# An AdaLN-style recurrence with a quantised feed-forward on one core: the first input tiles and the last output tile in halves

## What is computed

```python
# conditioning: a recurrence over time; the program runs it over T = 2048 steps, batch 2
xW = einsum('ntd,dh->nth', x, Wx) + b
next_h = tanh(xw_t + prev_h @ Wh)            # h0 = cond, 512 wide

# feed-forward on all hidden states, quantised on the fly
xq = clip(round(x / s), 0, 255) * s          # s = max(x) / 255
wq = clip(round(w / s_w), -128, 127) * s_w   # s_w = max|w| / 127 for each output row
bq = round(b / (s * s_w)) * (s * s_w)
h = relu(einsum(xq, w1q) + b1q)              # 512 -> 2048
y = einsum(hq, w2q) + b2q                    # 2048 -> 512, h quantised in the same way
return x + y
```

## Time and profile before

| | us |
|---|---|
| median of 3 runs | 501.66 |
| lowest, highest | 497.53, 505.16 |
| the profiled execution | 500.23 |
| its span, from the first to the last instruction | 498.2 |

### The profile page before, as it was taken

How to read it: one execution, slowest core, us unless ns; L and a number is a source line. 1 busy time by engine, 2 the same in 40 slices (tenths; PEclk the granted TensorE clock), 3 DMA queues, 4 the chain that set the end, 5 groups by cost and what they waited for, 6 DMA issues and landing times.

```text
span 498.2 us, 8921 instructions
## 1 busy us (share of the span) xinstructions
PE 479.3 (96%) x3004; PEld 327.6 (66%) x3004; DVE 293.8 (59%) x511; ACT 243.5 (49%) x451; POOL 92.1 (18%) x69
## 2 busy tenths in 40 slices
PE   8999999999999999999669999999998999999996
PEld 3678888888999999999654444444443444444442
DVE  2798556458233354545779877778787343454442
ACT  0326454454233232323673555555545567766761
POOL 2833290400000000000000000000001344434244
PEclk9999999999999999999899999999998999999999
DMA  8974422200457000000002777000002189878883
GB/s 292 387 255 170 169 86 86 84 1 1 95 108 135 0 1 0 0 0 0 2 1 87 293 298 314 24 0 0 0 1 86 51 293 311 301 268 314 300 318 119
DMA packets 38167, 65.40 MB, mean 131 GB/s; under 512 B 19056, under 2 KB 19200, under 8 KB 34560
## 3 DMA queue, kind: packets, MB, share of 16 engines
q1 hardware_dynamic: 37472, 64.04, 37.5%
q10 hardware_dynamic: 576, 1.05, 0.6%
q0 software_dynamic: 96, 0.01, 0.0%
HBM read 39.93 MB, written 20.97 MB: 122 GB/s over the span
## 4 chain that ended last, share of the span: by engine, by line
PE 87%; DVE 7%; DMA 2%; issue 1%; ACT 1%; SPq 1%; DVEq 0%
PE bank L850 22%; PE bank L789 22%; PE bank L579 14%; PE bank L616 12%; PE bank L622 11%; PE bank L606 3%; DMA arena<-w 2%; PE bank L642 2%; DVE arena L1179 2%; DVE arena L1318 1%; ACT arena L1049 1%; DVE w_absmax L1172 1%; PE bank L569 1%; DVE late_max L1525 0%; SPq L419 0%
## 5 line engine op out<-in xcount | busy, mean ns | idle before, releaser
L555 POOL TENSOR_SCALAR arena<-arena,bq 128x512 f32<-128x512 f32 x32 | 49.8, 1574 | 343.2 <-DVEq L1595 284.9
L789 PE MATMUL bank<-arena,w_words 128*128 128x512 f16 (+1 forms) x512 | 110.7, 379 | 0.7 <-DVE arena L1416 0.7
L850 PE MATMUL bank<-arena,w2t 128*128 128x512 f16 x512 | 111.1, 379 | 0.0
L789 PEld LDWEIGHTS bank<-arena,w_words 128*128 128x128 f16 x512 | 50.0, 98 | 61.0 <-DVE arena L1416 1.5
L850 PEld LDWEIGHTS bank<-arena,w2t 128*128 128x128 f16 x512 | 49.5, 98 | 61.5 <-DVE arena L1572 2.5
L1505 DVE TENSOR_REDUCE acc_max<-arena 128x2 f32<-128x1024 f32 x60 | 72.3, 1217 | 20.1 <-ACT arena L1105 19.1
L1105 ACT COPY arena<-bank 128x1024 f32<-128x1024 f32 x56 | 56.7, 1012 | 44.6 <-PE bank L789 44.6
L1125 ACT ACTIVATE arena<-arena,bias,scale 128x512 uint16 (+1 forms) x93 | 69.0, 804 | 8.7 <-PE bank L850 6.6
L616 PE MATMUL bank<-arena 128*128 x512 | 63.5, 277 | 0.0
L622 PE MATMUL bank<-arena 128*128 x512 | 62.4, 275 | 0.0
L616 PEld LDWEIGHTS bank<-arena 128*128 128x128 f32 x512 | 59.7, 192 | 0.6 <-issue 0.4
(11 more groups left out here) (111 smaller groups left out, 378.3 us busy)
## 6 DMA issues: line engine op xcount, KB each, us to landing
spill<-arena SPq DMA_DIRECT2D x12, 1024.0 KB, 3.9
arena<-spill SPq DMA_DIRECT2D x12, 1024.0 KB, 7.9
arena<-w SPq DMA_DIRECT2D x8, 1024.0 KB, 5.3
arena<-x_t SPq DMA_DIRECT2D x32, 256.0 KB, 3.9
y_t<-arena SPq DMA_DIRECT2D x32, 256.0 KB, 2.1
arena<-x_t SPq DMA_DIRECT2D x7, 1024.0 KB, 8.2
arena<-x_t ACTq DMA_DIRECT2D x4, 256.0 KB, 5.7
arena<-wx SPq DMA_DIRECT2D x4, 256.0 KB, 5.2
```

The lines of the kernel that those rows point to most:

```text
L555: nc.gpsimd.tensor_scalar(xb[:, d], xb[:, d], bq2[:, d:d + 1], None, ALU.add).then_inc(xb_ready, 1)
L789: mm = nc.tensor.matmul(bank[:, f % 8, :], w1t[:, k, f * P:(f + 1) * P], states_in[:, k, :], start=(k == 0), stop=(k == KT - 1))
L850: return nc.tensor.matmul(bank[:, 4 + d, :], w2t[:, f, d * P:(d + 1) * P], hq[:, f % HQ_RING, :], start=(f == 0), stop=(f == FT - 1))
```

## The change

The first tile (k = 0) of Wx and of the first x group is loaded as two transfers of 256 columns each, with a semaphore for each half. TensorE multiplies the first half of the columns of x with all four parts of the Wx tile, then the second half. It makes five idle products instead of seven. At the end, the last group's products stand behind the loop (now of seven turns) as a copy of their own, in which the fourth output tile is accumulated as two halves of 256 columns, in banks 7 and 3; its last three products of the first half come before those of the second. VectorE scales and SP stores each half by itself.

```diff
+HALF_BANKS = (7, 3)
-IDLE_START = 7
+IDLE_START = 5
@@ SyncE
-            for k in range(KT):
+            for j in range(2):
+                nc.sync.dma_start(wx_sb[:, 0, j * HALF:(j + 1) * HALF],
+                                  wx_v[0, :, j * HALF:(j + 1) * HALF]).then_inc(wx_first[j], 16)
+            for k in range(1, KT):
                 nc.sync.dma_start(wx_sb[:, k, :], wx_v[k]).then_inc(wx_in[k], 16)
...
-            store(GROUPS - 1)
+            store(GROUPS - 1, KT - 1)
+            for half in range(2):
+                sp.wait_ge(y_ready, Y_RING + GROUPS * KT + half)
+                cols = slice(half * HALF, (half + 1) * HALF)
+                nc.sync.dma_start(yT_v[tokens(GROUPS - 1), KT - 1, :, cols],
+                                  xb[:, KT - 1, cols]).then_inc(y_stored[KT - 1], 16)
             for d in range(KT):
-                sp.wait_ge(y_stored[d], 16 * GROUPS)
+                sp.wait_ge(y_stored[d], 16 * (GROUPS + (d == KT - 1)))
@@ TensorE
-            for k in range(KT):
+            for t in range(2):
+                pe.wait_ge(x0_first[t], 16)
+                for j in range(KT):
+                    if t == 0 and j % 2 == 0:
+                        pe.wait_ge(wx_first[j // 2], 16)
+                    nc.tensor.matmul(bank[:, j, t * HALF:(t + 1) * HALF], wx_sb[:, 0, j * P:(j + 1) * P],
+                                     x_in[:, X_ORDER[0], 0, t * HALF:(t + 1) * HALF],
+                                     start=(t == 0), stop=False, skip_group_check=True)
+            for k in range(1, KT):
                 pe.wait_ge(wx_in[k], 16)
                 pe.wait_ge(x0_in[k], 16)
...
-            def second_product(g, f, d):
-                return nc.tensor.matmul(bank[:, 4 + d, :], w2t[:, f, d * P:(d + 1) * P],
-                                        hq[:, f % HQ_RING, :], start=(f == 0), stop=(f == FT - 1))
+            def second_product(g, f, d, split=False, halves=(0, 1)):
+                weights = w2t[:, f, d * P:(d + 1) * P]
+                if not split or d < KT - 1:
+                    return nc.tensor.matmul(bank[:, 4 + d, :], weights, hq[:, f % HQ_RING, :],
+                                            start=(f == 0), stop=(f == FT - 1))
+
+                for half in halves:
+                    mm = nc.tensor.matmul(bank[:, HALF_BANKS[half], 0:HALF], weights,
+                                          hq[:, f % HQ_RING, half * HALF:(half + 1) * HALF],
+                                          start=(f == 0), stop=(f == FT - 1))
+                return mm
...
-                for d in range(KT):
+                for d in range(KT - 1 if split else KT):
...
+                if split:
+                    for half in range(2):
+                        for f in range(FT - TOGETHER, FT):
+                            mm = second_product(g, f, KT - 1, split, halves=(half,))
+                        mm.then_inc(last_half, 1)
...
-            with pe.Fori(0, GROUPS) as g:
+            with pe.Fori(0, GROUPS - 1) as g:
                 second_products(g)
+            second_products(GROUPS - 1, split=True)
@@ ScalarE
-            for k in range(KT):
+            for t in range(2):
+                nc.scalar.dma_start(x_in[:, X_ORDER[0], 0, t * HALF:(t + 1) * HALF],
+                                    x0_v[0, :, t * HALF:(t + 1) * HALF]).then_inc(x0_first[t], 16)
+            for k in range(1, KT):
                 nc.scalar.dma_start(x_in[:, X_ORDER[0], k, :], x0_v[k]).then_inc(x0_in[k], 16)
@@ VectorE
-            for k in range(KT):
+            for j in range(2):
+                dve.wait_ge(wx_first[j], 16)
+            for k in range(1, KT):
                 dve.wait_ge(wx_in[k], 16)
...
-            output(GROUPS - 1, range(KT), last=True)
+            output(GROUPS - 1, range(KT - 1))
+            dve.wait_ge(xb_ready, GROUPS * KT)
+            for half in range(2):
+                dve.wait_ge(last_half, half + 1)
+                cols = slice(half * HALF, (half + 1) * HALF)
+                nc.vector.scalar_tensor_tensor(
+                    out=xb[:, KT - 1, cols], in0=bank[:, HALF_BANKS[half], 0:HALF],
+                    scalar=s2_bits[:, KT - 1:KT], in1=xb[:, KT - 1, cols], op0=ALU.mult,
+                    op1=ALU.add).then_inc(y_ready, 1)
```

More of the change, by code:

```diff
@@ L281, in rnn_ffn_program @@
         bank = ctx.enter_context(nc.psum_tensor("bank", [P, 8, 512], F32))
+        wx_first = [sem(f"wx_first{j}") for j in range(2)]
+        x0_first = [sem(f"x0_first{t}") for t in range(2)]
         wx_in = [sem(f"wx_in{k}") for k in range(KT)]
@@ L364, in rnn_ffn_program @@
         y_acc = sem("y_acc")
+        last_half = sem("last_half")
         y_half = sem("y_half")
@@ L489, in fetch, with store @@
                                       spill[s, :, n * piece:(n + 1) * piece]).then_inc(fetched[n], 16)
-            def store(g):
-                for d in range(KT):
+            def store(g, tiles=KT):
+                for d in range(tiles):
                     sp.wait_ge(y_ready, Y_RING + g * KT + d + 1)
@@ L664, in _ @@
                     mm = nc.tensor.matmul(bank[:, j, :], wx_sb[:, k, j * P:(j + 1) * P],
-                                          x_in[:, X_ORDER[0], k, :], start=(k == 0),
-                                          stop=(k == KT - 1))
+                                          x_in[:, X_ORDER[0], k, :], start=False,
+                                          stop=(k == KT - 1), skip_group_check=True)
                     if k == KT - 1:
@@ L858, in wait_hidden, with opening_products @@
                     pe.wait_ge(relu_ready, g * (FT - len(OWN)) + f - mine + 1)
-            def opening_products(g):
+            def opening_products(g, split):
                 for f in range(2):
@@ L870, in opening_products, with last_products @@
                 for f in range(2):
-                    second_product(g, f, KT - 1).then_inc(hq_used, 1)
-            def last_products(g):
-                for d in range(KT):
+                    second_product(g, f, KT - 1, split).then_inc(hq_used, 1)
+            def last_products(g, split):
+                for d in range(KT - 1 if split else KT):
                     for f in range(FT - TOGETHER, FT):
@@ L884, in last_products, with second_products @@
                         mm.then_inc(y_acc, 1)
-            def second_products(g):
-                opening_products(g)
+                if split:
[3 more added lines that the diff above has]
+                        mm.then_inc(last_half, 1)
+            def second_products(g, split=False):
+                opening_products(g, split)
                 for f in range(2, FT - TOGETHER):
@@ L890, in second_products @@
                     for d in range(KT):
-                        mm = second_product(g, f, d)
+                        mm = second_product(g, f, d, split)
                     mm.then_inc(hq_used, 1)
-                last_products(g)
-            with pe.Fori(0, GROUPS) as g:
+                last_products(g, split)
+            with pe.Fori(0, GROUPS - 1) as g:
                 second_products(g)
+            second_products(GROUPS - 1, split=True)
         @block.scalar
@@ L1544, in _, with output @@
                                     ALU.mult).then_inc(scales1_ready, 1)
-            def output(g, tiles, last=False):
+            def output(g, tiles):
                 for d in tiles:
                     dve.wait_ge(xb_ready, g * KT + d + 1)
-                    if d == KT - 1 and not last:
+                    if d == KT - 1:
                         dve.wait_ge(y_half, 1 + g + 1)
@@ L1554, in output @@
                         continue
[L1555 to L1558, removed]
+                    dve.wait_ge(y_acc, g * (KT - 1) + d + 1)
                     nc.vector.scalar_tensor_tensor(
```

## The result

| | median us | lowest, highest | runs |
|---|---|---|---|
| kernel before | 503.65 | 497.53, 506.20 | 22 |
| changed kernel | 505.93 | 503.05, 507.54 | 22 |

The ratio is 1.0074, interval 1.0049 to 1.0099: the changed kernel is slower, by 0.7%, within the 2% that I had forecast. (A ratio here is an estimate over the runs and not the quotient of the two medians; it can lie some tenths of a percent away from it.) The median of 505.93 us is outside my range (499.2 to 505.6). I had worked out +1.06 us; the medians are 2.3 us apart, the plain means (502.82 and 505.66) 2.8, and the ratio stands for 3.7. The kernel before, too, is not what its first three runs showed: of its 22 runs, 11 lie from 497.5 to 503.0 and 11 from 504.3 to 506.2. The changed kernel has no run under 503.

A forecast was written before the change was run, and what follows sets the result against it. The prediction took the chain from w1's first block through VectorE to p3(1), then TensorE, as the bound. Adding +0.96 us (collisions) and +0.1 (tail) to the 501.66 median gave 502.7 us, range 499.2 to 505.6.

The forecast's parts named there:

- What bounds the kernel: Early chain: w1's first block lands at 14.86, VectorE quantises, add_11(1) releases TensorE, which waits 0.89 us at p3(1).
- A start at 4.0, δ = 0.45: Head: TensorE starts 0.9 us earlier than 4.89; δ, its work's forward shift up to p3(1), is 0.45 us, bounds 0 and 0.55.
- ε: Head: delay of the landing of w1's first block caused by the split loads, 0.1 us, bounds 0 and 0.5.
- The collisions: Second block: each L1179 beginning after GpSimd's x_sums(3) starts costs 1.41 us, others 0.40; two collide, +0.96 us, chance 0.38.
- r: Second block: δ + ε, forecast 0.55; one collision under 0.22, two from 0.22 to 0.61, three from 0.61 to 1.0.
- my 35.7: Forecast start of p3(1) on TensorE, instead of 34.76, after a wait of 2.3 us.
- The clock: Rival: a gap at the start or the 2.3 us wait at p3(1) halves TensorE's clock, +1.7 us; chance 0.10.
- the four-collision case: Rival's extreme at the second L1179: all four operations collide with GpSimd, 4.23 − 0.5, giving 505.5 us.
- The tail: Kernel end: moving the last stores' 1 MB sets the end, so halving the last output tile costs +0.1 us.
- Hidden: Rival at the head: halves land hardly earlier, r under 0.22, giving 501.6 us; chance 0.27.
- first meeting turned: Rival in the first block: VectorE's L1179 starts before x_sums(2), one collision goes, −1.2 us, giving 500.4; chance 0.13.
- three or more collisions: Slower rival at the second L1179: r passes 0.61, +2.4 us to 504.1, at most 505.5; chance 0.12.

The follow-up runs named there:

- e1: Kernel before with only the head of the change (first tiles in halves, five idle products), old tail: 505.87 us, ratio 1.0051.
- e4: Kernel before with first tiles loaded in halves, but TensorE waiting for all four and multiplying whole tiles after seven idle products: 505.77 us, ratio 1.0045.
- e5: Changed kernel with GpSimd's x_sums(3) also waiting for add_11(1): 501.49 us, ratio 0.9983 to the kernel before.
- e6: Changed kernel with 22 more idle products on TensorE ahead of p3(1): 502.62 us, ratio 0.9977 to the kernel before.
- e2: Kernel before with only the tail of the change (last output tile in halves, last group unrolled): 505.39 us, ratio 1.0033.
- e3: Kernel before with five idle products instead of seven, loads whole: 500.83 us, ratio 0.9965.
- e9: Kernel before with GpSimd's x_sums(3) also waiting for add_11(1): 498.42 us, ratio 0.9913.
- e13: Kernel before with only x's first tile loaded in halves, products whole; one run for its trace, VectorE's first look at w1's block at 15.24.
- e16: Kernel before with all eight tiles of Wx and first x loaded in halves by columns, products whole; one run for its trace, w1's block at 16.64.
- e8: Kernel before with the first block of w1 issued ahead of x group 1 instead of behind it: 505.29 us, ratio 1.0080.

## Why the prediction was wrong

**What bounds the kernel: right.** The chain through the landing of w1's block, VectorE and p3(1) is what the change acted on, in its own trace and in those of e1, e4, e5 and e6.

**A start at 4.0, δ = 0.45: near.** 3.75 was measured, and a δ of 0.85, since the pace also rose earlier than in the earlier trace rows: the sixteen halves take 4.99 us from 3.75 to 8.74, 1.4 more than the 3.62 of sixteen at full pace, which is 2.7 us at half pace, until 6.5 or so and not 7.3 (an estimate from these rows). I had taken the moment of the rise to be fixed by one trace; in the traces of the kernel before, e2 and e3 the first group's 32 products take 15.17, 13.97 and 16.61 us from the same start.

**The landing of the block, ε = 0.1 with an upper bound of 0.5: the step that failed.** It measured 1.94, and over all traces with such halves 1.2 to 2.2. I had bounded it by SP's issue and by the size of the rows, with the reasoning that full queues lie ahead. SP did issue the block only 0.75 us later (5.22 after 4.47). The queues are full from 3.5 us on in the kernel before (shares of 1.01 and 1.04 in the two stages above), and they aren't when the first transfers are small (0.73 and 0.56). A bound that rests on "the engines are busy then" was taken from the very stretch that the edit changes. The two rows of the trace that could have warned stood in the earlier trace rows: from 1.5 to 3.5 us the engines moved 141 and 209 GB/s, so in that stretch neither bytes nor issue time were the limit.

**The collisions: right as a mechanism.** The steps of 1.41 and 0.40 us, the thresholds in r and the anchor at GpSimd's start were borne out by e2 (four collisions, 37.66 against 37.8 worked out), e3 (none) and e5, e9 (taken away). e13 is by chance the very case that I forecast: GpSimd starts at 32.10 and the four at 31.63, so r is 0.54 (0.20 + 0.34). Two collide, the four take 3.69 us, and TensorE waits 2.4 us where I had 2.3. But in the changed kernel, with ε at 1.94, r is 2.8, beyond every case that I priced. There not only L1217 collides, but L1212 before it (1.27 us instead of 0.17), and VectorE's end is no longer tied to GpSimd's start as my formula has it. Of the 2.8 us by which p3(1) is later than my 35.7 (38.53), the landing is 1.94. The added collisions cost 1.8 us where my sum has 1.41, and the 0.45 by which GpSimd's earlier start was to bring VectorE's end forward does not appear.

**The clock: the term that was left out of the sum.** I put TensorE's wait at 2.3 us and the fall of the clock among the rivals, at +1.7. The wait was 5.5 us, the fall lasted 6.8 us, and it cost 2.8 us; e6, where it is gone, is 3.3 us faster. With p3(1) 3.8 us later and this, the sum is 6.6 before anything comes back.

**The base.** I set the forecast on the median of three runs and on a profiled execution of 500.23, and called the spread of the runs something "by themselves". It is most likely this mechanism: in the kernel before, small differences in TensorE's first microseconds decide how many L1179 collide, and then whether the clock falls. That half of its runs have what the changed kernel nearly always has is an inference from three traces and from e9, where the long runs are gone; not every run has a trace. Had I priced the four-collision case as something the kernel before already does, I would have read two groups of runs, at 500 and at 505, out of 497.53, 501.66 and 505.16.

**The tail: near.** +0.1 forecast; +0.2 in the traces, with the DMA engines full until about 1 us before the end, as forecast.

**The chances.** Within 2% at 0.96 was right. "Hidden" and "first meeting turned" did not occur; three or more collisions, to which I gave 0.12, comes closest.

## What to carry to other kernels

Before making an engine start earlier, find who else it releases, and what those then run beside: here TensorE's 0.85 us were handed back at the next wait, while one wait that keeps GpSimd out of VectorE's way was worth 0.9%, and two of them 1.1% in the kernel before. When the runs of a kernel spread by more than 1%, look for a wait near the point where the clock falls, and compare two traces from the two ends of the spread before forecasting any edit. A transfer at the start of a kernel should be costed by what lands behind it, not by its own bytes.

## What the runs showed of the hardware

- Splitting the first of four 256 KB tiles on two queues brought TensorE's first product to 3.75 us instead of 4.89 and put the 1 MB block behind them 1.9 us later (1.7 over twelve traces, from 1.2 to 2.2), with DMA engines at 0.56 busy in between; splitting all four tiles put it no later than that (16.64, e16).
- A VectorE tensor_scalar on 128x4 elements (a maximum and a product) took 1.27 us instead of 0.17 when it began 0.02 us after an operation of GpSimd: it ended with that operation, whatever its own size. A reciprocal on as many elements, begun beside GpSimd's next operation, took 0.18 us as ever.
- TensorE idle for 5.0 to 5.5 us on this core brought a granted clock of 0.50 for 6.8 us (changed kernel, e1, e2, e8, e16) and in e4 (5.3 us) for 3.4; a wait of 2.7 us brought 3.4 us of it (e5), one of 2.4 us (e13) and one of 1.1 (e9) none.
